# Counting a graph's edges on TensorE: blocks of 7 to 11 targets instead of 17, four visits marked at once

## What is computed

```python
def gnn_layer(x, W, b, src, dst):
    h = x @ W.T + b
    agg = jax.ops.segment_sum(h[src], dst, num_segments=1250)
    return jax.nn.relu(agg)

xn = layernorm(x)
x = x + gnn_layer(gnn_layer(xn, W1, b1), W2, b2) + linear_attention_mix(xn, Wq, Wk, Wv, mW1, mW2)
x = x + routed_experts(layernorm(x))      # Sinkhorn gates, top-156 of 1250 nodes for each of 8 experts
```

## Time and profile before

| | |
|---|---|
| median of 3 timed runs | 470.88 us (470.62 to 471.15) |
| span of the profiled execution | 468.7 us |
| TensorE busy in the span | 449.7 us (96%) |
| VectorE busy | 320.8 us (68%) |
| ScalarE, GpSimd busy | 150.6, 62.2 us |
| mean granted clock of TensorE | 0.997 of full speed |

### The profile page before, as it was taken

How to read it: one execution, slowest core, us unless ns; L and a number is a source line. 1 busy time by engine, 2 the same in 40 slices (tenths; PEclk the granted TensorE clock), 3 DMA queues, 4 the chain that set the end, 5 groups by cost and what they waited for, 6 DMA issues and landing times.

```text
span 468.7 us, 6795 instructions
## 1 busy us (share of the span) xinstructions
PE 449.7 (96%) x2418; PEld 361.1 (77%) x2418; DVE 320.8 (68%) x1102; ACT 150.6 (32%) x271; POOL 62.2 (13%) x89
## 2 busy tenths in 40 slices
PE   6999999999999999999999999999999999778995
PEld 3888788888888888888879999877777776554783
DVE  6995799899998988897652110444645657777972
ACT  4686453322323333342222110322132115551120
POOL 4088200000000000000004000002200000005642
PEclk9999999999999999999999999999999999999998
DMA  8902002911000000001200000002744449206791
GB/s 218 283 3 90 1 0 91 217 47 68 2 1 1 1 1 1 1 2 36 91 0 3 1 1 1 1 0 79 269 140 134 133 140 384 105 1 214 264 352 73
DMA packets 20828, 40.45 MB, mean 86 GB/s; under 512 B 2936, under 2 KB 3266, under 8 KB 20787
## 3 DMA queue, kind: packets, MB, share of 16 engines
q1 hardware_dynamic: 18547, 32.55, 22.4%
q0 software_dynamic: 2240, 7.39, 4.3%
HBM read 30.10 MB, written 10.30 MB: 86 GB/s over the span
## 4 chain that ended last, share of the span: by engine, by line
PE 85%; DVE 8%; ACT 3%; issue 1%; DMA 1%; SPq 0%; POOLq 0%; DVEq 0%; ACTq 0%
PE ps L717 46%; PE ps L1007 9%; PE ps L939 9%; PE ps L830 5%; PE ps L704 5%; ACT scrap_a L1382 2%; PE ps L1133 2%; PE ps L1024 1%; DMA X<-in_x 1%; PE ps L1103 1%; PE ps L862 1%; PE ps L751 1%; PE ps L966 1%; PE ps L988 1%; PE ps L1046 1%
## 5 line engine op out<-in xcount | busy, mean ns | idle before, releaser
L1671 DVE TENSOR_SCALAR RING_D<-places,PLACES 125x170 bf16<-125x170 f16 (+1 forms) x239 | 62.7, 262 | 0.0
L1672 DVE TENSOR_SCALAR RING_S<-iota,HOME 125x128 bf16<-125x128 f16 x239 | 59.6, 249 | 0.0
L939 PE MATMUL ps<-AT,H1L 125*128 125x416 f32 (+1 forms) x108 | 38.0, 352 | 0.0
L939 PE MATMUL ps<-AT,H1H 125*128 125x416 f32 (+1 forms) x108 | 38.0, 352 | 0.0
L1007 PE MATMUL ps<-H2H,AT 125*125 125x512 f32 x90 | 36.2, 402 | 0.0
L1007 PE MATMUL ps<-H2L,AT 125*125 125x512 f32 x90 | 35.5, 395 | 0.0
L1024 PE MATMUL ps<-WE0H 128*128 128x512 f32 x125 | 34.2, 408 | 0.0
L1739 DVE TENSOR_TENSOR ps<-ps,bias 125x512 f32<-125x512 f32 x20 | 14.0, 700 | 27.9 <-PE ps L717 27.9
L1818 DVE SCALAR_TENSOR_TENSOR ZL<-ps,ZH 128x416 fp32r<-128x416 f32 (+1 forms) x12 | 6.3, 585 | 38.7 <-ACT ZH L1335 38.7
L704 PEld LDWEIGHTS ps<-RING_D,RING_S 125*125 125x125 bf16 x239 | 25.7, 137 | 7.9
L596 POOL TENSOR_TENSOR G2L<-RAW_G,G2H 128x512 fp32r<-128x512 f32 x4 | 5.0, 1299 | 192.2 <-ACT G2H L1152 192.2
(11 more groups left out here) (402 smaller groups left out, 1176.5 us busy)
## 6 DMA issues: line engine op xcount, KB each, us to landing
RAW_E<-in_experts SPq DMA_DIRECT2D x8, 1024.0 KB, 9.8
RAW_AGAIN<-in_experts SPq DMA_DIRECT2D x3, 1024.0 KB, 10.6
X<-in_x SPq DMA_DIRECT2D x1, 2240.0 KB
out_x<-X SPq DMA_DIRECT2D x10, 224.0 KB
scratch<-X SPq DMA_DIRECT2D x10, 224.0 KB
scratch<-Y SPq DMA_DIRECT2D x10, 224.0 KB
RAW_K<-in_WkT SPq DMA_DIRECT2D x4, 256.0 KB, 4.9
RAW<-in_mW2T SPq DMA_DIRECT2D x1, 1024.0 KB, 12.6
```

Source lines behind the costliest of these rows:

```text
L939: pe.matmul(place(f), h[0:TT, k, 128 * f:128 * (f + 1)], AT[0:TT, k, c0:c1], start=(k == 0 and n == 0), stop=False)
L1671: V.tensor_scalar(hot_d(v, width(b)), places[0:ET, 0:width(b)], PLACES[0:ET, c:c + 1], None, ALU.is_equal)
L1672: V.tensor_scalar(hot_s(v), iota[0:ET, :], HOME[0:ET, c:c + 1], None, ALU.is_equal).then_inc(done["marked"], 1)
```

## The change

Targets are cut into 125 blocks of 7 to 11 (`RUNS`: number of blocks, width, visits each), which need 322 visits. A group is as many whole blocks as fit 510 columns; there are 28 instead of 25. Visits are handled in batches of four (`BATCH`), one batch per spot: 80 of four and one of two. VectorE marks a whole batch with two `tensor_tensor` operations: `every_place` and `every_home`, tiles on GpSimd's account that hold every number four times in a row, against four columns of `PLACES` and `HOME`, broadcast. In the result the visit is the innermost index, so a visit's product reads every fourth element, in the stationary tile (now all 128 columns) and in the moving one (70 to 110 columns). `HOME` and `PLACES` become 16-bit. The rings hold 2 and 5 batches. The selection becomes one operation over all blocks and one per run; its columns now stand in the order of the visits. GpSimd's small constants (`turns`, `start`) move behind two of its splits of WK, and the table `first` is written with one iota per run; `every_home` and `every_place` follow it. The warm-up tile is 1000 elements, `zero` is filled only in `count_again`, and `gw1`, `below` and others lie elsewhere.

```diff
-W = 17
-VISITS = [20, 10, 8, 7] + [6] * 3 + [5] * 5 + [4] * 17 + [3] * 45
+RUNS = [(1, 11, 16), (1, 9, 7), (2, 10, 6), (3, 11, 5), (5, 11, 4), (7, 9, 3), (20, 11, 3), (23, 8, 2), (13, 9, 2),
+        (10, 10, 2), (39, 11, 2), (1, 9, 1)]
-RING_A, RING_B = 6, 16
+BATCH = 4
+RING_A, RING_B = 2, 5
...
     for k, (unit, n) in enumerate(spots):
+        vs = range(BATCH * k, min(BATCH * (k + 1), NV))
...
+        MARK_S = small("MARK_S", [128, RING_A, 128, BATCH], BF16, "a")
+        MARK_D = small("MARK_D", [128, RING_A, HOTD, BATCH], BF16, "a")
+        RING_S = at("RING_S", [128, RING_B, 128, BATCH], BF16, 125)
+        RING_D = at("RING_D", [128, RING_B, HOTD, BATCH], BF16, 130)
...
-                    pe.wait_ge(done["marked"], v + 1)
-                    pe.matmul(PS[4 + g % 2][0:TT, o:o + width(b)], hot_s(v)[:, 0:TT], hot_d(v, width(b)), start=(s == 0),
-                              stop=(s == VISITS[b] - 1), skip_group_check=True).then_inc(done["visited"], 1)
+                    if v % BATCH == 0:
+                        pe.wait_ge(done["marked"], k + 1)
+                    mm = pe.matmul(PS[4 + g % 2][:, o:o + width(b)], hot_s(k)[:, :, v % BATCH], hot_d(k, width(b))[:, :, v % BATCH],
+                                   start=(s == 0), stop=(s == VISITS[b] - 1), skip_group_check=True)
+                    if v % BATCH == BATCH - 1 or v == NV - 1:
+                        mm.then_inc(done["visited"], 1)
...
-                        V.tensor_scalar(hot_d(v, width(b)), places[0:ET, 0:width(b)], PLACES[0:ET, c:c + 1], None, ALU.is_equal)
-                        V.tensor_scalar(hot_s(v), iota[0:ET, :], HOME[0:ET, c:c + 1], None, ALU.is_equal).then_inc(done["marked"], 1)
+                    V.tensor_tensor(hot_d(k, w), every_place[0:ET, 0:w], PLACES[0:ET, c].unsqueeze(1).broadcast_to([ET, w, BATCH]),
+                                    ALU.is_equal)
+                    V.tensor_tensor(hot_s(k), every_home[0:ET], HOME[0:ET, c].unsqueeze(1).broadcast_to([ET, 128, BATCH]),
+                                    ALU.is_equal).then_inc(done["marked"], 1)
...
+                link(V.scalar_tensor_tensor(place_in[0:TP], ps, 1.0, touch[0:TP], ALU.add, ALU.mult))
+                for b, v, count, _, visits in run_starts():
+                    shape = [TP, 2, count, visits]
+                    ins = V.tensor_tensor(SEL[0:TP, :, v:v + count * visits].rearrange("p h (b s) -> p h b s", s=visits),
+                                          place_in[0:TP, :, b:b + count].unsqueeze(3).broadcast_to(shape),
+                                          places[0:TP, 0:visits].unsqueeze(1).unsqueeze(1).broadcast_to(shape), ALU.is_equal)
```

More of the change, by code:

```diff
@@ L165, in psum_plan, with target_groups @@
     return uses
[L168 to L185, removed]
-ORDER = [(b, s) for b in range(NB) for s in range(VISITS[b])]
+def target_groups():
+    found, lo = [], 0
+    for b in range(NB + 1):
+        if b == NB or NT * (EDGES[b + 1] - EDGES[lo]) > HOTW:
+            found.append((lo, b))
+            lo = b
+    assert EDGES[NB] == N
+    return found
@@ L189, in visits_in_products, with run_starts @@
+GROUPS_OF_TARGETS = target_groups()
+NG = len(GROUPS_OF_TARGETS)
+GROUP_OF = [g for g, (lo, hi) in enumerate(GROUPS_OF_TARGETS) for _ in range(lo, hi)]
+ORDER = [(b, s) for b in range(NB) for s in range(VISITS[b])]
+def run_starts():
+    b, v, found = 0, 0, []
+    for count, w, visits in RUNS:
+        found.append((b, v, count, w, visits))
+        b, v = b + count, v + count * visits
+    return found
 def visits_in_products():
-    spots = [("vp0", 6, 3)]
+    spots = [("vp0", 6)]
     for u in ("vp1", "vp2", "vp3", "cp0", "cp1", "cp2", "cp3"):
-        spots += [(u, n, 3) for n in (0, 6)]
+        spots += [(u, n) for n in (0, 6)]
@@ L195, in visits_in_products @@
     for i in range(NT + 1):
         if i < NT:
[L197 removed]
+            spots += [(f"q{i}", n) for n in (0, 6)]
         if i:
[L199 to L206, removed]
@@ L207, in visits_in_products @@
-    assert v == NV
-    return found
[L211 to L227, removed]
+            spots += [(f"x{i - 1}", n) for n in (0, 6, 12, 18)]
+    spots += [(f"h{i}", 6) for i in range(NT)]
@@ new lines, in visits_in_products, with ring_slot, slot_free @@
+    found = []
+    for k, (unit, n) in enumerate(spots):
+        vs = range(BATCH * k, min(BATCH * (k + 1), NV))
+        if vs:
+            found.append((unit, n, vs))
+    assert len(found) * BATCH == NVB
+    return found
+BATCHES = visits_in_products()
+VISITS_AT = {(unit, n): vs for unit, n, vs in BATCHES}
+IN_A = next(k for k, (unit, n, _) in enumerate(BATCHES) if (unit, n) == ("q0", 6)) + 1
+def ring_slot(k):
+    return k % RING_A if k < IN_A else RING_A + (k - IN_A) % RING_B
+def slot_free(k):
+    if k < IN_A:
+        return max(k - RING_A + 1, 0)
+    return max(k - RING_B + 1, 0) if k - IN_A >= RING_B else 0
@@ L327, in gps_block @@
[L327 to L335, removed]
+        HOME = small("HOME", [128, NVB], F16, "a")
@@ new lines, in gps_block @@
+        PLACES = small("PLACES", [128, NVB], F16, "a")
+        every_home = small("every_home", [128, 128, BATCH], F16, "a")
+        every_place = small("every_place", [128, HOTD, BATCH], F16, "a")
+        ring = areas["a"][0] / KB
+        keys = at("keys", [128, 3, 2, ET], F16, ring)
+        edge = at("edge", [128, 2, 2, ET], F32, ring + 1.5)
+        below = at("below", [128, NB], F32, ring)
+        HOT_S = at("HOT_S", [128, AGAIN, 128], BF16, ring)
+        HOT_D = at("HOT_D", [128, AGAIN * HOTW], BF16, ring + 0.5)
@@ L336, in gps_block @@
+        turns = small("turns", [128, NB], F16, "a")
+        over = small("over", [128, 1], F32, "p")
+        grp = small("grp", [128, 2, 2], F32, "k")
         eps = small("eps", [128, 2], F32, "a")
-        zero = small("zero", [128, 128], BF16, "a")
+        zero = at("zero", [128, 128], BF16, 122.5)
         stat = small("stat", [128, NT, 6], F32, "a")
@@ L818, in chosen_tiles @@
                     for n in (1, 2):
-                        mm = pe.matmul(ps, keys[0:TP, n, h, :], SEL[0:TP, h, :], start=(h == 0 and n == 1), stop=(h == 1 and n == 2))
+                        mm = pe.matmul(ps, keys[0:TP, n, h, :], SEL[0:TP, h, 0:NV], start=(h == 0 and n == 1), stop=(h == 1 and n == 2))
                 closes("keys", mm)
@@ L1774, in count_again @@
                 rounds = NE_T // AGAIN
+                after("visited", len(BATCHES))
+                link_again(V.memset(zero[:], 0.0))
                 dve.sem_inc(done["again_go"], 1)
```

144 lines of the change are left out of this document (68 added, 76 removed).

## The result

The changed kernel takes 480.18 us (480.17 to 480.34, 4 runs), the kernel before 470.93 beside it; the ratio is 1.019 (95% interval 1.016 to 1.022). The profiled execution has a span of 478.5 us against 468.7. The forecast was 476.3.

What follows compares the result with a forecast made beforehand. It took TensorE's own time to pass the visits as the bound. Visits +5.2 and ranks and choice +0.2 gave +5.4 us on the 468.7 us span, 474.1; with 2.2 for timed runs, 476.3 us. Range 466 to 480.5.

Steps and rivals of the forecast that it cites:

- the step s: Time between visits inside a batch on TensorE: 0.088 us, 241 of them 21.2 us; break-even at 0.066.
- the 0.9: Moving column at 8 bytes, if 1.8 ns is paid once for two neighbours: 0.9 ns, step 0.097 us, +7.4 us.
- the 0.72 by the bytes from 20: Moving column cost if it goes with bytes swept, 8/20 of 1.8 ns: 0.72 ns, step 0.079 us, +3.0 us.
- 81 ends of 0.10 us: From a batch's last visit to the resumed products on TensorE: 0.10 us for each of 81 batches, 8.1 us.
- the 5.2 forecast: Visits on TensorE: 8.1 + 21.2 = 29.3 us after the change against 24.1 before, +5.2 us.
- The 0.065 us that it read for a 90-column step: In the old kernel's last two visits, a 125-column stationary load sets a pace of some 0.06 us.
- The load of the new stationaries costs nothing: Loading stationary marks 8 bytes apart fits under 0.035 us, below any step considered, so it adds 0.
- One of its signs: In the trace, load records of 128 columns would be no longer than the visits' step.
- Ranks and choice: Wider fp32 ranks products, mostly covered by TensorE's 0.31 us wait, +0.13; six wider choice products, 0.08; together +0.2 us.
- no wait at the banks: Twelve plain products and a batch, 3.1 us, cover ScalarE's 0.589 us counts copy; rival: waits, 482 us, 5%.
- Full rate at 8 bytes: Rival, 27%: moving columns 8 bytes apart stream as if contiguous, step 0.048 us, visits 19.7 us, time 466.7 us.
- The 1.8 ns column: Rival, 3%: two columns being near saves nothing in the moving read, 1.8 ns a column, 508 us.

Runs made afterwards that it cites:

- the late tables: Changed kernel with GpSimd's `every_home` and `every_place` written only after VectorE's last operation on the keys: 481.18 us, ratio 1.019.
- the one with early tables: Changed kernel with GpSimd's `every_home` and `every_place` written ahead of its wait for the last MP product: 481.16 us, ratio 1.022.
- with one and with both halves altered: Changed kernel with a visit's marks side by side: moving only 535.86 us, stationary only 561.37, both 688.88.

## Why the prediction was right, and where its sum was short

**Direction and mechanism: right.** It said that all hangs on the step s, that TensorE has no gap, and that VectorE's saving buys nothing. 80-column batches step shorter than 110-column ones, and no matmul in the stretch waits for marks or counts. (The loads of 15 batches wait up to 0.3 us for marks, and these batches start no later than the others: 0.006 us behind a plain step against 0.005.)

**The step, +0.8 us.** 0.0911 us instead of 0.088, times 241. The column costs 0.87 ns; of the two estimates that were averaged, the 0.9 ("1.8 ns is paid once for two neighbouring columns") was right, and the 0.72 by the bytes from 20 was not, since at 20 bytes the cost is already at its top (1.73 at 16). No row told the two apart, so that their middle came within 4% is in part luck.

**The end of a batch: the step that failed in the visits, +2.7 us.** The prediction took "81 ends of 0.10 us" from contiguous visits and held them fixed, though it let the other 241 visits read with a step. An end is 0.134 (0.005 ahead of the first visit and 0.129 behind the last); 81 x 0.034 = 2.7. Not all of it is the step. By the starts of all chunks, the ends before were 0.107 already. Of the other 0.027, 0.009 lie ahead of the first visit and come with 128 stationary columns (0.004 with the marks side by side as well, -0.003 with 125), and 0.018 behind the stepped read. With the 0.4 us that the visits before cost beyond the 24.1 of the sum (24.5 by the mean of all chunks), the difference is 0.8 + 2.7 - 0.4 = 3.1 above the 5.2 forecast: 8.3, and the traces show 8.15. The 0.065 us that it read for a 90-column step was a wrong split, too: the two starts lie 0.043 us apart, and 0.122 of the 0.165 are the rest. With 125 columns side by side the floor shows in the later steps (0.058 for the third).

**The load: nearly right, by its condition.** "The load of the new stationaries costs nothing" holds for the pace with 128 columns; a batch is 0.02 us longer by it, 1.7 us for 81 batches as an estimate from five, which is contained in the two terms above. One of its signs did not come: load records (120 ns) are longer than the visits' step (91), and the steps go by the moving read all the same. With 125 at 8 bytes it would have been the bound, 0.46 us a batch.

**Ranks and choice: +0.13 and +0.08 forecast, +1.23 and +0.07 found.** The choice's six products came as forecast (they lie in the row of +0.37, the rest of which was not followed). The ranks' products grew as computed: 62.94 - 1.13 - 60.59 = 1.22 us from the first ranks product to the wait, 0.41 more than the 1.12 - 0.31 before. But the 0.31 us of waiting that were to cover them grew to 1.13. The prediction had placed GpSimd's tables only by GpSimd's own idle time and had not asked whom they hold up on VectorE. With the late tables the ranks cost 0.16, close to its 0.13.

**The rest.** Marks (forecast 0.42 and 0.39 us), copies of the counts at 0.548 us, no wait at the banks, XNL not later: right. The start came out 0.63 us earlier, which no run explains; the altered kernels, but for the one with early tables, reach the ranks anywhere from 60.41 to 61.99 us, so one trace on each side doesn't tell it from scatter. Timed runs lie 1.7 us above the span, not 2.2.

**Rivals.** Full rate at 8 bytes fell with the steps; its condition, a column under 0.59 ns, is met at 4 bytes, and there the kernel does go to 470, not to that rival's 466.7: the steps (0.053), the ends (0.113) and the ranks cost more than it had for them. The 1.8 ns column exists at 16 bytes: 507 us, close to that rival's 508. The range held the time by 0.3 us, and that is luck: the visits were 3 us short, the ranks 1.1 and the rows of +0.37 and +0.59 together 0.9, while the earlier start and the smaller distance between span and time gave back 1.1.

## What to carry to other kernels

A layout that makes the writer cheap can make the reader dear: price both sides, and change the layout first on paper for the engine that has no gap. A constant read off one access pattern (here the end of a chunk) is not a constant under another. Work put into one engine's idle time is free only if it shares nothing with a neighbour that is on the path at that moment.

## What was not expected of the hardware

VectorE's 16-bit writes at a distance of 256 bytes cost 4.8 to 5.4 ns an element (2479 and 2765 ns for 512, with one and with both halves altered) against 0.8 side by side. The difference of 0.29 us comes from the operation ahead: the marks of homes take 0.29 us longer behind stepped marks of places even when they are themselves written as before (706 against 419 ns). Holding one operand over the innermost index costs 1.3 (687 for 512). 125 stationary columns side by side set a floor of 0.28 us for four visits at any width, 128 do not.
